# Attention scores by pairs of heads: both plain fp32 products first, then both heads' fp32r products

## What is computed

```
xn = layernorm(x)
q, k, v = xn @ wq, xn @ wk, xn @ wv      # 32 query heads, 8 key/value heads, 128 wide; rope on q and k
scores = q k^T * 128**-0.5               # position i sees j with i-128 < j <= i
s = (softmax(scores) @ v) @ wo
g = silu(ffn(xn))                        # gated FFN, 1376 hidden units, 4-bit packed weights
out = x + s * g
```

## Time and profile before

| | |
|---|---|
| median of 3 runs | 878.67 us (878.37 to 880.2) |
| the profiled execution | 877.86 us |
| its span, first to last instruction | 876.1 us |
| TensorE matmul records busy | 840.6 us, 96% of the span |
| TensorE weight loads busy | 701.8 us, 80% |
| VectorE / ScalarE / GpSimd busy | 600.6 / 469.7 / 390.2 us |
| mean granted TensorE clock | 0.998 of full speed |

### The profile page before, as it was taken

One profiled execution on the slowest core, in us unless ns is written; L12 is line 12 of the kernel. 1 busy time (PEld: TensorE's weight loads), 2 busy tenths in 40 slices (PEclk: granted clock), 3 DMA queues, 4 the chain that ended last, 5 costly groups with the idle time before them and its releaser, 6 DMA issues.

```text
span 876.1 us, 13995 instructions
## 1 busy us (share of the span) xinstructions
PE 840.6 (96%) x4252; PEld 701.8 (80%) x4252; DVE 600.6 (69%) x1621; ACT 469.7 (54%) x1133; POOL 390.2 (45%) x303
## 2 busy tenths in 40 slices
PE   3999999999989999999999999999999999999887
PEld 3777888888767888888888888888888888888765
DVE  7953554433569677775968586677858676875895
ACT  2474121132577557574756666485748557574641
POOL 0144121124545436552644464184435436552892
PEclk9999999999999999999999999999999999999999
DMA  6200001002010201200120111012000201200211
GB/s 195 56 18 8 13 24 51 19 1 72 1 41 9 74 1 48 73 1 1 48 72 0 48 36 35 0 48 72 0 27 21 72 0 48 72 0 0 61 62 60
DMA packets 40224, 32.55 MB, mean 37 GB/s; under 512 B 5056, under 2 KB 32384, under 8 KB 40192
## 3 DMA queue, kind: packets, MB, share of 16 engines
q1 hardware_dynamic: 40192, 32.16, 12.5%
HBM read 30.05 MB, written 2.10 MB: 37 GB/s over the span
## 4 chain that ended last, share of the span: by engine, by line
PE 82%; DVE 8%; POOL 3%; issue 3%; ACT 3%; DMA 0%; SPq 0%; ACTq 0%; POOLq 0%; DVEq 0%
PE bank L966 25%; PE bank L968 24%; PE bank L967 24%; PE bank L1106 5%; PE bank L1086 3%; DVE probs L815 2%; POOL acc L338 1%; ACT W2raw L433 1%; POOL swap L321 1%; PE bank L986 1%; PE bank L1076 1%; DVE xl L655 1%; POOL acc L342 0%; POOL q L325 0%; DMA xn<-in_L_attn_x 0%
## 5 line engine op out<-in xcount | busy, mean ns | idle before, releaser
L321 POOL TENSOR_TENSOR swap<-swap,cst 128x512 f32<-128x512 f32 x80 | 103.9, 1298 | 248.8 <-ACT swap L488 247.9
L966 PE MATMUL bank<-xh,wih 128*128 128x512 f32 x384 | 158.5, 413 | 0.2 <-DVE q L783 0.2
L968 PE MATMUL bank<-xh,wil 128*128 128x512 f32 x384 | 151.0, 393 | 0.0
L967 PE MATMUL bank<-xl,wih 128*128 128x512 f32 x384 | 150.3, 391 | 0.0
L815 DVE TENSOR_SCALAR probs<-probs,rinv 128x128 f32<-128x128 f32 (+1 forms) x256 | 129.1, 546 | 4.6
L515 ACT ACTIVATE probs<-probs,nmx 128x128 f32<-128x128 f32 (+1 forms) x256 | 113.5, 445 | 33.8 <-DVE nmx L804 33.4
L523 ACT ACTIVATE ph<-bank 128x512 fp32r<-128x512 f32 x96 | 55.6, 597 | 112.2 <-PE bank L1106 110.9
L966 PE MATMUL bank<-woh,oh 128*128 128x512 f32 x256 | 100.4, 392 | 0.3 <-DVE ol L832 0.3
L968 PE MATMUL bank<-woh,ol 128*128 128x512 f32 x256 | 99.9, 390 | 0.0
L967 PE MATMUL bank<-wol,oh 128*128 128x512 f32 x256 | 99.9, 390 | 0.0
L287 POOL TENSOR_TENSOR hl<-act_h,hh 128x512 fp32r<-128x512 f32 x22 | 29.9, 1361 | 148.2 <-ACT hh L416 148.2
(11 more groups left out here) (102 smaller groups left out, 1828.0 us busy)
## 6 DMA issues: line engine op xcount, KB each, us to landing
raw<-in_L_attn_wq SPq DMA_DIRECT2D x32, 256.0 KB, 2.8
raw<-in_L_attn_wo SPq DMA_DIRECT2D x32, 256.0 KB, 2.9
packed<-in_L_ffn_w SPq DMA_DIRECT2D x20, 128.0 KB, 2.2
xn<-in_L_attn_x SPq DMA_DIRECT2D x8, 256.0 KB, 3.5
raw<-in_L_attn_wk SPq DMA_DIRECT2D x8, 256.0 KB, 3.0
raw<-in_L_attn_wv SPq DMA_DIRECT2D x8, 256.0 KB, 2.7
raw<-in_L_attn_x SPq DMA_DIRECT2D x8, 256.0 KB, 2.7
out<-gate SPq DMA_DIRECT2D x8, 256.0 KB, 2.0
```

Source lines behind the costliest of these rows:

```text
L321: nc.gpsimd.tensor_tensor(v, v, spread(sin.unsqueeze(1), P, 2, SEQ), ALU.mult).then_inc(sin_done, 1)
L966: nc.tensor.matmul(out_, sh, mh, start=(i == 0), stop=False)
L967: nc.tensor.matmul(out_, sh, ml, start=False, stop=False)
L968: m = nc.tensor.matmul(out_, sl, mh, start=False, stop=(i == n - 1))
```

## The change

`scores` now serves two heads, `h0` and `h0 + 1`. It issues the plain fp32 product of the first, the plain fp32 product of the second, then the three fp32r products of the first (which raise `scores_ps`) and those of the second. The waits in front of each product are the same as before; they now stand in the new order. The calls are merged two by two. Nothing changes on the other engines, and the number of instructions on TensorE is the same.

```diff
-            def scores(g, bp, b, h):
-
-                s = 4 * b + h
-                if b == 0:
-                    pe.wait_ge(rope_done, cnt(5, g, bp, h + 2))
-                wait(pe, masked, cnt(8, g, bp, s - 1))
+            def scores(g, bp, b, h0):
+
                 c = b * SEQ
-                nc.tensor.matmul(S_B[s % 2][:, 0:P], q[:, h, c:c + P], k[:, bp, c:c + P], start=True, stop=True)
-                if b == 0:
-                    pe.wait_ge(klq_done, cnt(5, g, bp, h + 2))
-                three(S_B[s % 2][:, P:3 * P], [(qh[:, h, b, :], ql[:, h, b, :], kh[:, bp, c:c + SEQ],
-                                                kl[:, bp, c:c + SEQ])]).then_inc(scores_ps, 1)
+                for h in (h0, h0 + 1):
+                    s = 4 * b + h
+                    if b == 0:
+                        pe.wait_ge(rope_done, cnt(5, g, bp, h + 2))
+                    wait(pe, masked, cnt(8, g, bp, s - 1))
+                    nc.tensor.matmul(S_B[s % 2][:, 0:P], q[:, h, c:c + P], k[:, bp, c:c + P], start=True, stop=True)
+                for h in (h0, h0 + 1):
+                    if b == 0:
+                        pe.wait_ge(klq_done, cnt(5, g, bp, h + 2))
+                    three(S_B[h % 2][:, P:3 * P], [(qh[:, h, b, :], ql[:, h, b, :], kh[:, bp, c:c + SEQ],
+                                                    kl[:, bp, c:c + SEQ])]).then_inc(scores_ps, 1)
...
             scores(0, 0, 0, 0)
-            scores(0, 0, 0, 1)
             project(0, 1, 0)
             scores(0, 0, 0, 2)
-            scores(0, 0, 0, 3)
             project(0, 1, 1)
...
                 scores(g, bp, 1, 0)
-                scores(g, bp, 1, 1)
                 project(ng, nbp, 2)
                 scores(g, bp, 1, 2)
-                scores(g, bp, 1, 3)
...
```

More of the change, by code:

```diff
@@ L1193, in step @@
                     scores(ng, nbp, 0, 0)
-                    scores(ng, nbp, 0, 1)
                 out_project(g, bp, 0)
                 scores(ng, nbp, 0, 2)
-                scores(ng, nbp, 0, 3)
                 if last:
@@ L1200, in step @@
                     scores(ng, nbp, 1, 0)
-                    scores(ng, nbp, 1, 1)
                     out_project(g, bp, 2)
                     scores(ng, nbp, 1, 2)
-                    scores(ng, nbp, 1, 3)
                     return
```

## The result

The changed kernel takes 881.87 us, the median of 9 runs (880.17 to 883.91), against 878.67 us for the kernel before (9 runs, 877.99 to 880.49). The ratio is 1.0036, with a 95% interval from 1.0024 to 1.0048: it is slower by some 3 us. The forecast was 881.5 us.

What follows compares the result with a forecast made beforehand. The prediction took TensorE to bound the kernel. Stalls of 2.2 us plus 0.6 us in the first half, less 0, added 2.8 us to the profiled 877.86, giving 880.7, or a median of 881.5 us; range 876.5 to 884.5.

Steps and rivals of the forecast that it cites:

- The bound: Regular part, 296.5 to 809.5 us: TensorE has 512.98 us of matmul in 513.00, so any new wait is paid at once.
- A change of type costs nothing: At every pair, going from fp32 to fp32r was priced at nothing; the upper bound was 0.08 us each.
- the short 0.14 us in front and the long 0.20 us behind: Matmul start spacings around the type change: time missing before it reappears after, 0.23 us for two passes.
- Fourteen stalls of 0.16 us, 2.2 us: Heads 2 and 3 of `b = 0`, regular part: head 3's load waits for head 1's masking, bounds 0 to 4.2 us.
- The signal's 0.12 us: Time from the end of VectorE's masking read to the TensorE load it releases, measured in the first half.
- The first half, 0.57 us: Heads 2 and 3 there: head 2's fp32r passes come after head 3's wait, delaying the first transposes 0.57 us.
- the rivals: Type change costs 0.08 us (876.4 us, chance 0.14); stall smaller or partly repaid (0.29); VectorE's lateness reaches TensorE (885 us, 0.09).
- The last half costs nothing: Head 2's three passes (0.35 us) fit in the 1.5 us between two waits; without that cover, 0.35 us once.
- VectorE's lateness is hidden: At `b = 1`, VectorE gets 0.23 us late in about 7 halves, covered by 0.78 us less 0.12; uncovered, 1.6 us.
- The sum: Whole kernel: 2.2 + 0.6 - 0 = 2.8 us slower; 2 to 4 us slower had chance 0.48.

Runs made afterwards that it cites:

- e7: Changed kernel with VectorE's masking of heads 0 and 1 of `b = 0` ahead of the step's last `o_lo`: 880.25 us, ratio 1.0020.
- e3: Kernel before with pairs ordered fp32r, fp32 of the first head, then fp32, fp32r of the second; one type change, second head's waits as before: 878.87 us, ratio 1.0006.
- e6: Changed kernel with two spare fp32 products per pair, one behind each of the first head's first two fp32r products: 906.92 us, ratio 1.0317.
- e5: Changed kernel with two spare fp32 products per pair, together directly behind the two real fp32 ones: 908.00 us, ratio 1.0331.
- e1: Changed kernel with the old order kept at heads 2 and 3 of `b = 0`, so new order at 48 pairs: 878.62 us, ratio 0.9996.
- e4: Changed kernel with TensorE's second group written out instead of run in the loop: 882.34 us, one run.
- e9: Kernel before with the new order only at heads 2 and 3 of the first half, one pair: 881.28 us, ratio 1.0021.
- e2: Kernel before with the new order only at heads 2 and 3 of `b = 0`, 16 pairs: 880.99 us, ratio 1.0027.
- e8: Kernel before with, in the first half, VectorE's first masking ahead of the last `kq_lo` and ScalarE's first exponential ahead of the last `kq_hi`: 877.85 us, ratio 0.9993.
- e11: Kernel before with the reordered start of e8 and the first normalise also ahead of the last `kq_lo`: 877.80 us, ratio 0.9988.
- e10: Changed kernel with the masking order of e7 and the first half's VectorE and ScalarE orders of e8: 879.71 us, ratio 1.0004.

## Why the prediction was right, point by point

**The bound.** TensorE without slack in the regular part: right. A stall of 0.07 us at a place moved the whole rest of the kernel by as much, and e7 gave it back.

**A change of type costs nothing:** right, and shown three ways: pairs without a stall keep 1.16 us (e3 and the changed kernel), three changes in a pair cost no more than one (e6 against e5), and e1 is level. The reading by which the short 0.14 us in front and the long 0.20 us behind are one and the same pass held.

**Fourteen stalls of 0.16 us, 2.2 us:** right in place and cause, and the one term that was sized wrong: 0.03 to 0.13 us each, 1.0 us in all, by the trace; 1.4 us by the difference of the ratios of the changed kernel and e7, with wide intervals. The distance to the read was nearly as forecast, 0.09 to 0.16 us with a mean of 0.13, where the same count gives 0.10 to 0.17 and 0.15 for the kernel before. The signal's 0.12 us was what failed. It came from the first half, which is written out; e4 shows that the wait is passed some 0.07 us sooner in the loop, where twelve of the fourteen are.

**The first half, 0.57 us:** right at full clock (0.53 in e4), and short by half of what the profile of the changed kernel shows, 1.1, since TensorE's clock then ran at half. The trace of before had the wait that precedes it, but no row at the lower clock there, and the possibility was not among the rivals. It could have been: the same trace has half clock between 822 and 826 us, behind a wait of 2.47 us.

**The last half costs nothing:** right. Its second pair takes 2.84 us in both traces.

**VectorE's lateness is hidden:** right. Head 2 of `b = 1` is taken up 1.00 us into the pair (382.69 for the pair at 381.69 us) where it was 0.78 or 0.79 in the halves where VectorE had waited, and the pairs behind are no later for it.

**The sum** of 2.8 us against 3.2 measured was met in part by luck: in the trace the stalls are 1.2 us less than the sum had, the first half 0.5 us more, and 0.9 us of creep was not in the sum at all. The late half clock seems to have no part in it: the times of both kernels fall into two groups as e9's do, and the medians differ by 3.2 us within each (881.6 against 878.4, and 883.5 against 880.3).

## What to carry to other kernels

Before instructions are regrouped to save a cost that a profile seems to show, look at the weight loads' starts: where they are evenly spaced across the supposed cost, it is an effect of how matmuls are drawn. Regrouping brings the later group's waits forward; list each moved wait with the time at which its signal came before, and price those that come within the distance moved. Take a signal's travelling time from the same kind of code, loop or written out, in which the wait will stand. Where an effect is no larger than what the clock can take, 2 us here, look at how the single times fall into groups before reading a difference of medians.

## What the runs showed of the hardware

A plain fp32 product of 128 columns takes 0.22 us, as two passes of 0.11, whether fp32r matmuls stand around it or not. The fp32r matmul behind it is recorded 0.08 us too long and the pass before it as much too short.

A wait in the written-out part of TensorE's code cost some 0.07 us more than in its loop, 1.30 against 1.20 to 1.24 us a pair.

Half the granted clock (1.2 GHz) for about 3 us followed a wait of 1.75 us and a gap of 0.27 us in the loads, in four executions out of five (the changed kernel, e2, e7 and e9; not e4). Behind the same wait without the gap it was absent in three (before, e1, e3). A gap is not needed: behind a wait of 2.43 to 2.53 us near 825 us (850 in e5 and e6), which all thirteen traces have, the clock was at half for some 3 us in nine of them, before included, and at full in e1, e5, e8 and e11. A late stretch of 7 us at half clock cost 2.0 us, 33.2 against 31.2 us from the last pair of scores to the end.

Half a dozen matmuls of 512 columns behind a pair ran 0.228 to 0.236 us apart instead of 0.227, some 0.03 us in all. Behind heads 0 and 1 of `b = 1` this is so in every trace in which the two plain fp32 products stand one behind the other there (the changed kernel, e1, e4 to e7, e10, and e3 with its other order) and in none in which they stand apart (before, e2, e8, e9, e11). It comes to 0.4 to 0.7 us over thirteen halves in e1, e3 and e7. But the same spacing is in the trace of before behind heads 2 and 3 of `b = 0` (0.02 us each) and behind every second pair of heads 0 and 1 of `b = 0` in the loop, so the order of the products is not the only thing that brings it. No run here shows why.
